# Router weights and routing masks with their low parts beside the high ones, in a macaron transformer layer

## What is computed

```
x = x + 0.5 * ffn(layernorm(x))
x = x + attention(layernorm(x))
x = x + 0.5 * ffn(layernorm(x))
```

```
gate_logits = einsum('bsd,ed->bse', x, gate_w)        # 8 logits a row
topw, sel = top_k(gate_logits, 2)
topw = softmax(topw, axis=1)                           # over the sequence axis
for e in range(8):
    c = sum(where(sel == e, topw, 0))
    h_e = silu(base_up + lo_up[e]) * (base_gate + lo_gate[e])
    mixed_h += c * h_e ;  lora_down += 2 * (c * h_e @ down_A[e].T @ down_B[e].T)
out = mixed_h @ w_down.T + lora_down
```

## Time and profile before

| | |
|---|---|
| median of 3 runs | 1437.02 us (1436.83 to 1437.51) |
| the profiled execution's own time | 1436.71 us |
| its span in the trace | 1434.9 us |
| PE busy | 1389.6 us (97%), 8164 matmuls |
| DVE, POOL, ACT busy | 1011.2 us (70%), 929.6 us (65%), 903.5 us (63%) |

### The profile page before, as it was taken

The page is one execution under the profiler, slowest core; times in us unless marked ns, Lnnn a source line. Parts: engine busy times, 40 slices in busy tenths (PEclk is TensorE's granted clock), DMA queues, the critical chain, the costliest instruction groups (busy, mean ns, idle before and its releaser), DMA issues.

```text
span 1434.9 us, 24075 instructions
## 1 busy us (share of the span) xinstructions
PE 1389.6 (97%) x8164; PEld 1214.6 (85%) x8164; DVE 1011.2 (70%) x2207; ACT 903.5 (63%) x1826; POOL 929.6 (65%) x818
## 2 busy tenths in 40 slices
PE   6999999889999999999999999999999988999998
PEld 4778888678999998998999899989999977878886
DVE  6877776867766766766766767766776788766665
ACT  4554443667777877777777767776776764544433
POOL 3665454477777877777777777777777744745543
PEclk9999999999999999999999999999999999999999
DMA  4000001000000000000000000000000030000000
GB/s 172 1 1 1 1 1 52 23 1 9 23 2 8 23 2 8 23 2 8 22 2 9 1 23 9 1 23 1 8 9 1 2 114 1 0 16 1 16 15 15
DMA packets 11415, 23.29 MB, mean 16 GB/s; under 512 B 928, under 2 KB 5024, under 8 KB 11168
## 3 DMA queue, kind: packets, MB, share of 16 engines
q1 hardware_dynamic: 11296, 21.78, 4.5%
HBM read 19.68 MB, written 2.10 MB: 15 GB/s over the span
## 4 chain that ended last, share of the span: by engine, by line
PE 85%; DVE 7%; POOL 4%; issue 2%; ACT 1%; DMA 0%; DVEq 0%; POOLq 0%; ACTq 0%
PE ps L1602 25%; PE ps L1604 25%; PE ps L1603 25%; PE ps L2011 8%; POOL um_l L356 1%; POOL hid_l L356 1%; DVE mixed L1218 1%; DVE hid L1208 1%; POOL w_l L356 0%; POOL mixed_l L356 0%; PE ps L1615 0%; DVE ps L1462 0%; DVE stats L1063 0%; DVE xn L1082 0%; DVE spread L1082 0%
## 5 line engine op out<-in xcount | busy, mean ns | idle before, releaser
L720 POOL TENSOR_SCALAR probs<-probs,inv_sum 128x128 f32<-128x128 f32 (+7 forms) x256 | 197.7, 776 | 210.6 <-DVE inv_sum L1447 210.6
L1462 DVE CUSTOM_DVE_ANT_0 ps<-ps,causal 128x128 f32<-128x128 f32 (+7 forms) x256 | 194.3, 759 | 125.1 <-PE ps L1604 124.7
L999 ACT ACTIVATE probs<-ps,neg_max 128x128 f32<-128x128 f32 (+7 forms) x256 | 189.4, 740 | 136.6 <-DVE neg_max L1462 136.3
L356 POOL TENSOR_TENSOR hid_l<-hid,hid_h 128x512 fp32r<-128x512 f32 x80 | 109.4, 1368 | 184.2 <-ACT hid_h L836 184.2
L2011 PE MATMUL ps<-ident,probs 128*128 128x128 f32 x1152 | 169.9, 274 | 7.6 <-DVE own_l L356 3.1
L704 POOL TENSOR_TENSOR rot_sin<-swapped,rope 128x512 f32<-128x512 f32 x128 | 165.5, 1293 | 17.8 <-ACT swapped L947 10.7
L710 POOL TENSOR_TENSOR rot<-rot,rot_sin 128x512 f32<-128x512 f32 x124 | 160.2, 1292 | 17.8
L2011 PEld LDWEIGHTS ps<-ident,probs 128*128 128x128 f32 x1152 | 133.1, 141 | 24.1 <-issue 3.8
L1602 PE MATMUL ps<-k_h,q_h 128*128 128x384 f32 (+5 forms) x384 | 151.0, 393 | 2.4 <-DVE q_l L356 2.4
L356 DVE TENSOR_TENSOR own_l<-ps,own_h 128x128 fp32r<-128x128 f32 (+3 forms) x256 | 124.0, 484 | 38.4 <-ACT own_h L970 38.4
L1604 PE MATMUL ps<-k_h,q_l 128*128 128x384 f32 (+5 forms) x384 | 131.3, 342 | 0.0
(11 more groups left out here) (202 smaller groups left out, 4396.1 us busy)
## 6 DMA issues: line engine op xcount, KB each, us to landing
w_raw<-attn_w SPq DMA_DIRECT2D x32, 256.0 KB, 2.9
w_in<-ffn_w SPq DMA_DIRECT2D x12, 576.0 KB, 9.2
x_sb<-x_in SPq DMA_DIRECT2D x4, 512.0 KB, 6.2
out<-x_sb SPq DMA_DIRECT2D x3, 512.0 KB, 3.1
rope<-rope_w SPq DMA_DIRECT2D x1, 1024.0 KB, 6.4
w_in<-ffn_w SPq DMA_DIRECT2D x2, 264.0 KB, 4.6
expand_raw<-expand_w SPq DMA_DIRECT2D x2, 256.0 KB, 5.8
out<-x_sb SPq DMA_DIRECT2D x2, 256.0 KB, 2.1
```

The lines of the kernel that those rows point to most:

```text
L356: return eng.tensor_tensor(dst, src, high.bitcast(F32), ALU.subtract)
L720: pool.tensor_scalar(probs[s % 4][:, 0:n], probs[s % 4][:, 0:n], inv_sum[:, s % 4:s % 4 + 1], 1.0, ALU.mult, ALU.mult).then_inc(probs_read ...
L999: act.activation(probs[t % 4][:, 0:a * n].rearrange("p (a n) -> p a n", a=a), view, ACT.Exp, bias=neg_max[:, t % 4:t % 4 + 1], scale=-1.0, ...
L1462: dve.tensor_tensor_reduce(out=view, in0=view, in1=causal[:, SEQ - a * n:].rearrange("p (a n) -> p a n", a=a), scale=-SCALE, scalar=HUGE, ...
```

## The change

The router's columns stand twice in block 0: 8 columns whose high part is kept, and the same 8 again, which POOL overwrites with the low part, for each half of the model dimension. A matmul then gives eight rows of high logits and eight of low logits at once, so that a chunk takes four matmuls instead of eight; `turn_logits` turns 16 rows, and a new DVE reduction adds the two halves into `cm` before the top eight are taken. The masks are put into `cm_pad` twice; the transpose gives 64 rows, of which the second 32 become the low part, in one tile `maskT`. C1 and C2 take one matmul each, with 64 rows of weights. M1 and D take one each as before, but with 32 rows of weights where there were 128.

```diff
-OFF_A = KT * EXPERTS
+OFF_A = KT * 2 * EXPERTS
...
         def w_route(w, kt):
-            at = OFF_ROUTE + kt * EXPERTS
+            at = OFF_ROUTE + kt * 2 * EXPERTS
             return w[:, at:at + P]
+        def route_parts(w):
+            return w[:, OFF_ROUTE:OFF_A].rearrange("p (a b e) -> p a b e", a=KT, b=2)[:, :, 1, :]
...
+                if n == 0:
+                    low(pool, route_parts(w_h), route_parts(w_in), route_parts(w_h))
+                    at = slice(OFF_A, BLOCK0)
                 low(pool, w_l[:, at], w_in[:, at], w_h[:, at]).then_inc(w_ready, 1)
...
                 dve.wait_ge(logits_ready, 2 * f + b + 1)
+                at = 2 * EXPERTS * SEQ_TILES * b
+                halves = ps[:, TURNED_BANKS[f][b], at:at + 2 * EXPERTS * SEQ_TILES]\
+                    .rearrange("p (t h e) -> p t h e", t=SEQ_TILES, h=2)
+                dve.tensor_reduce(cm[:, of_batch(b), 0:EXPERTS], halves.rearrange("p t h e -> p t e h"), AX.X, ALU.add)\
+                    .then_inc(logits_summed, 1)
+                dve.wait_ge(logits_summed, 2 * f + b + 1)
...
             def pad_mask(g, c):
                 need(dve, mask_turned, g)
-                dve.tensor_copy(cm_pad[:, :, 0:MASK_ROWS], cm[:, ds(CT * c, CT), :]).then_inc(cm_padded, 1)
+                twice = cm_pad[:, :, 0:2 * MASK_ROWS].rearrange("p t (k r) -> p t k r", k=2)
+                dve.tensor_copy(twice, cm[:, ds(CT * c, CT), None, :].to_broadcast([P, CT, 2, MASK_ROWS]))\
+                    .then_inc(cm_padded, 1)
             def mask_low_part(g, bank):
                 dve.wait_ge(mask_high, g + 1)
-                low(dve, maskT_l[:], ps[:, bank, :], maskT_h[:]).then_inc(mask_low, 1)
+                rest = maskT[MASK_ROWS:2 * MASK_ROWS]
+                low(dve, rest, ps[MASK_ROWS:2 * MASK_ROWS, bank, :], rest).then_inc(mask_low, 1)
...
                 for kt in range(KT):
-                    product(ps[:, bank, :], (w_route(w_h, kt), w_route(w_l, kt)), xnT(kt, chunk_cols(c)), kt == 0, False)
-                    ins = pe.matmul(ps[:, bank, :], w_route(w_l, kt), xnT_l[:, kt, chunk_cols(c)], start=False,
+                    pe.matmul(ps[:, bank, :], w_route(w_h, kt), xnT_h[:, kt, chunk_cols(c)], start=(kt == 0), stop=False)
+                    ins = pe.matmul(ps[:, bank, :], w_route(w_h, kt), xnT_l[:, kt, chunk_cols(c)], start=False,
                                     stop=(kt == KT - 1))
...
                 if e < EX_C1:
-                    pe.matmul(ps[:, banks[e], :], expand[:, e], maskT_h[:], start=True, stop=True).then_inc(spread_done, 1)
+                    pe.matmul(ps[:, banks[e], :], expand[0:MASK_ROWS, e], maskT[0:MASK_ROWS], start=True, stop=True)\
+                        .then_inc(spread_done, 1)
                 else:
                     pe.wait_ge(spread_kept, 4 * g + e - 1)
-                    pe.matmul(ps[:, banks[e], :], expand[:, e], maskT_h[:], start=True, stop=False)
-                    pe.matmul(ps[:, banks[e], :], expand[:, e], maskT_l[:], start=False, stop=True).then_inc(spread_done, 1)
+                    both = slice(0, 2 * MASK_ROWS)
+                    pe.matmul(ps[:, banks[e], :], expand[both, e], maskT[both], start=True, stop=True).then_inc(spread_done, 1)
```

More of the change, by code:

```diff
@@ L188, in build @@
             hid = sbuf(st, "hid", [P, 2, CHUNK])
-            sbuf(st, "before_values", [P, 48])
+            sbuf(st, "before_values", [P, 32])
             cm_pad = sbuf(st, "cm_pad", [P, CT, P])
@@ L199, in build @@
             spread = sbuf(st, "spread", [P, 2, 4, CHUNK])
-            maskT_h = sbuf(st, "maskT_h", [P, CHUNK], F32R)
-            maskT_l = sbuf(st, "maskT_l", [P, CHUNK], F32R)
+            maskT = sbuf(st, "maskT", [P, CHUNK], F32R)
+            sbuf(st, "mask_gap", [P, CHUNK])
             um_h = sbuf(st, "um_h", [P, 2, 4, CHUNK], F32R)
@@ L281, in build @@
         logits_ready = sem("logits_ready")
+        logits_summed = sem("logits_summed")
         route_chain = sem("route_chain")
@@ L358, in logitsT @@
         def logitsT(c):
-            return spread[0:EXPERTS, 1, c % 2, :]
+            return spread[0:2 * EXPERTS, 1, c % 2, :]
         def rope_low_part(eng, index, u, k):
@@ L772, in keep_logits @@
                 act.wait_ge(logitsT_done, 4 * f + c + 1)
-                act.activation(logitsT(c), ps[0:EXPERTS, LOGIT_BANKS[f][c], :], ACT.Copy).then_inc(logitsT_kept, 1)
+                act.activation(logitsT(c), ps[0:2 * EXPERTS, LOGIT_BANKS[f][c], :], ACT.Copy).then_inc(logitsT_kept, 1)
             def layer_norm_high(n, c, banks=(OUT0, OUT1), kts=range(KT)):
@@ L782, in mask_high_part @@
                 act.wait_ge(mask_turned, g + 1)
-                act.activation(maskT_h[:], ps[:, bank, :], ACT.Copy).then_inc(mask_high, 1)
+                act.activation(maskT[0:2 * MASK_ROWS], ps[0:2 * MASK_ROWS, bank, :], ACT.Copy).then_inc(mask_high, 1)
             def keep_spread(g, e, banks):
@@ L1106, in logits @@
                 def logits(tile):
-                    return ps[:, TURNED_BANKS[f][b], EXPERTS * tile:EXPERTS * tile + EXPERTS]
+                    return cm[:, tile, 0:EXPERTS]
                 dve.wait_ge(logits_ready, 2 * f + b + 1)
+                at = 2 * EXPERTS * SEQ_TILES * b
[4 more added lines that the diff above has]
+                dve.wait_ge(logits_summed, 2 * f + b + 1)
                 for tile in tiles:
@@ L1636, in turn_logits @@
                     for tt in range(CT):
-                        at = EXPERTS * (CT * c + tt)
-                        ins = pe.transpose(ps[:, TURNED_BANKS[f][b], at:at + EXPERTS], logitsT(c)[:, P * tt:P * tt + P],
-                                           ident[0:EXPERTS, 0:EXPERTS])
+                        at = 2 * EXPERTS * (CT * c + tt)
+                        ins = pe.transpose(ps[:, TURNED_BANKS[f][b], at:at + 2 * EXPERTS], logitsT(c)[:, P * tt:P * tt + P],
+                                           ident[0:2 * EXPERTS, 0:2 * EXPERTS])
                 ins.then_inc(logits_ready, 1)
@@ L1697, in turn_mask @@
                 for tt in range(CT):
-                    ins = pe.transpose(ps[:, bank, P * tt:P * tt + P], cm_pad[:, tt, :], ident[:])
+                    ins = pe.transpose(ps[0:2 * MASK_ROWS, bank, P * tt:P * tt + P], cm_pad[:, tt, 0:2 * MASK_ROWS], ident[:])
                 ins.then_inc(mask_turned, 1)
@@ L2141, in pack_ffn @@
     a = np.concatenate([up_A.reshape(ER, D).T, gate_A.reshape(ER, D).T], axis=1)
-    parts = [by_kt(gate_w.T), by_kt(a)]
+    parts = [by_kt(np.concatenate([gate_w.T, gate_w.T], axis=1)), by_kt(a)]
     for m in range(FULL):
@@ L2161, in expand_matrices @@
         m[EXPERTS + e, EX_D, ranks] = ALPHA
-        m[2 * EXPERTS + e, EX_C1, :] = 1.0
-        m[3 * EXPERTS + e, EX_C2, :] = 1.0
+        for part in (0, MASK_ROWS):
+            m[part + 2 * EXPERTS + e, EX_C1, :] = 1.0
+            m[part + 3 * EXPERTS + e, EX_C2, :] = 1.0
     return m.reshape(P, EX_COLS)
```

## The result

The changed kernel takes 1440.81 us (median of 10 runs, 1439.22 to 1441.21) beside 1436.76 us of the kernel before, measured with it (10 runs, 1435.96 to 1438.67). The ratio is 1.0026, 95% interval 1.0018 to 1.0034: slower by 4.05 us, clear of the noise, though the interval reaches down across the 0.2% that the prediction took as its line. The profiled execution took 1441.19 us, nearly the slowest of the ten, with a span of 1439.1, 4.2 more than the span of before.

What follows compares the result with a forecast made beforehand. PE was taken to bound the dense feed-forward stretches, with waits between engines at the two heads. The terms -2.23 - 1.86 + 4.41 + 0.14 made +0.46 us on 1437.02, so 1437.5 us, range 1430.0 to 1440.8.

Steps and rivals of the forecast that it cites:

- The likeliest case: Whole kernel: all terms as forecast, 1437.5 us, own range 1435.5 to 1439.0, chance 0.45; no change in all had 0.62.
- slower: Whole kernel above 1439.9 us, from dearer switches or the clock falling in both passes; chance 0.15.
- head of f = 0: First feed-forward pass's start: fewer router matmuls against a new reduction, copies and split subtraction; -2.23 us.
- head of f = 1: Second feed-forward pass's start: two groups of four router matmuls gain -0.93 us each, others vanish in waits; -1.86 us.
- spreads in six chunks: Inside six chunks: three excursions to fewer rows cost 1.20, two saved matmuls return 0.465; +0.735 each, +4.41 us.
- copy at chunk 1: Head of chunk 1, both passes: DVE's copy ahead of the second sequence's masks lies on the path; +0.14 us.
- The switches: PE in the chunks: changing between whole-array and fewer-row matmuls costs 0.20 us, there and back 0.40 us.
- free: Rival, spreads in the chunks: switches cost nothing, each chunk gains 0.465 us, total 1430.3 us; chance 0.14.
- half: Rival, spreads in the chunks: switches cost half, 18 x 0.20 us less, total 1433.9 us; chance 0.13.
- `router_logits(0, 3)` waits only 0.22 us and opens the dense stretch: Head of f = 0, last router product: four matmuls saved there count fully; -0.93 us.
- for the second sequence's reduction, DVE's own waits for PE in the dense stretches: Dense stretches: DVE's idle time hides the second reduction, cost 0; without this cover +0.27 us in each pass.
- The clock's rival: Both heads: longer PE waits drop the clock, slowing transposes and LoRA products; +1.2 to +3 us, 1438.7 to 1440.5, chance 0.20.

Runs made afterwards that it cites:

- run 3: The changed kernel with spreads inside the chunks over all 128 rows, zero-padded, still in one pass; 1433.82 us, ratio 0.9978 to the kernel before.
- run 8: The kernel before with M1 and D alone over 32 of 128 rows, no matmul removed; 1438.42 us, ratio 1.0008.
- run 12: The kernel before with both passes of C1 and C2 over 64 of 128 rows, no matmul removed; 1441.58 us, ratio 1.0033.
- Run 4: The changed kernel with PE waiting for the new reduction's end instead of the top-eight indices, in two places; 1437.79 us, ratio 1.0007 to the kernel before.
- run 11: The changed kernel plus 6 and 8 useless PE matmuls in waits at the two heads; 1438.76 us, ratio 1.0017 to the kernel before.
- run 5: The changed kernel with one-pass spreads over 128 rows and PE waiting for the reduction, not the indices; 1432.8 us, ratio 0.9971 to the kernel before.
- run 10: The kernel of run 5 plus 8 useless PE matmuls in the second head's wait alone; 1433.21 us, ratio 0.9969 to the kernel before.
- Run 6: The kernel before with eight more matmuls in a dense stretch (fourth chunk's M1 repeated), nothing else; 1438.65 us, ratio 1.0009.
- run 7: The kernel before with four more matmuls in the same dense stretch, nothing else; 1437.55 us, ratio 1.0003.
- both mends: The two edits of run 5 to the changed kernel: spreads over 128 rows, and PE waiting for the reduction; 1432.8 us.
- run 2: The kernel before with the changed masks and spreads alone, router as before; 1441.88 us, ratio 1.0035.
- run 1: The kernel before with the changed router alone, masks and spreads as before; 1434.56 us, ratio 0.9982.
- run 9: The kernel of run 5 plus 6 and 8 useless PE matmuls in waits at both heads; 1432.21 us, ratio 0.9967 to the kernel before.

## Why the prediction was right, and where it was not

The forecast of 1437.5 was 3.3 us low, and the time lies on the very edge of the range, which ended at 1440.8: that it falls inside is luck. The likeliest case said no change (0.62) and reached to 1439.0; what came was "slower", which had 0.15. The term that the prediction called decisive was right, the heads were not. By its own terms, against the two profiled executions:

| term | forecast | in the trace |
|---|---|---|
| head of f = 0 | -2.23 | -0.3 (0.53 at the landmark, less 0.735 for one chunk's spreads and 0.07 for the copy) |
| head of f = 1 | -1.86 | -1.7 (from 3.01 at 1177.74 to 2.14 at 1280.34, less 0.735 and 0.07) |
| spreads in six chunks | +4.41 | +4.49 (1.48 + 1.54 + 2 x 0.735) |
| copy at chunk 1 | +0.14 | taken as forecast |
| attention | 0 | +1.0 (from 2.01 at 218.64 to 3.01 at 1177.74) |
| end | 0 | +0.5 (3.68 at 1390.36 to 4.2) |
| sum | +0.46 | +4.2 |

**The switches: right, in mechanism and size.** "A switch takes some 0.09 us to let the array run empty and 0.11 us because the weights are loaded in the open", an excursion 0.40 us. Four ways of reading it agree: 1.10 us across C1 in after, 0.38 between run 3's landmarks, 0.375 from run 8's two chunks (0.75 / 2), and 1.32 us across C1 in run 12. It holds for 32 and 64 rows, though the price came from matmuls of 8 rows that are 8 columns long. That the price of such unlike matmuls would carry over this exactly was not known ahead (the bounds were 0 and 0.55); in part it is luck. The rivals "free" and "half" are excluded: run 12, which removes nothing and has 12 excursions, is 4.3 us slower, where half the price would make 2.4. The rule of the Trainium skill that the prediction named (TensorEngine Tiling (Array Packing), Key Properties), that a change of the tiling mode drains the engine, agrees with the traces at 32, 64 and 8 rows.

**The head of f = 0: the step that failed.** It is the term that priced eight matmuls at -1.86 and four at -0.93 "in the dense stretch" and let them count to the end. Up to `turn_mask` it held, though only against before's profiled execution (see the last section). Then it missed that the path leaves PE. First, "`router_logits(0, 3)` waits only 0.22 us and opens the dense stretch": what PE did earlier there, PE waited out at 53.32, since DVE's chain was released by products ahead of that router. Second, "for the second sequence's reduction, DVE's own waits for PE in the dense stretches" were named as its cover; there is none at this place, DVE works from 50.36 to 53.28 without a wait, and PE waits for the end. Run 4 takes the wait away and moves the landmark by 0.88 us. Third, the clock.

**The clock's rival (0.20): it came true in f = 0.** "The wait at 39.85 grows from 1.39", and the lower level behind it hits transposes and LoRA products: 1.25 us on DVE's path (run 11 against after), beside the 1.2 to 1.5 that the rival gave for one pass. The wait itself did not grow (1.39 us in both). In f = 1 it did not fall in after, but in run 3 it did. The traces of after and of runs 4 and 5 have this second low stretch, those of runs 3 and 10 don't, though they too have both parts of the change here; what decides it wasn't found. By the medians the router alone is 2.3 us faster and the spreads alone are 5.0 slower, which makes +2.6, and the whole change is +4.05. The other 1.4 us would fit this stretch and run 11 (-2.05), but they are not clear of the noise of three medians. In run 11's trace it is 1.25 us, and the rest of its lead over after comes from the start and from the attention.

**The head of f = 1: right** within 0.2 us. PE waited 1.87 us for DVE's rows (0.92 before), as said; it also waited 0.37 us for the second indices.

**What stays open.** In the profiled execution the attention and the last six matmuls (distance 0.21 instead of 0.12 us, granted clock 0.61) cost 1.5 us more. Runs 6 and 7 show that such a shift alone doesn't bring this cost in the median. What decides where the clock falls, at the first head as in the attention, wasn't settled. Nor was it tested what more than two matmuls of fewer rows in a row would cost.

## What to carry to other kernels

Fewer rows of weights are no saving for a lone matmul: padded with zeros to the shape of its neighbours, the same matmul is 0.4 us cheaper (512 columns, in a dense stretch). A saved matmul counts only if the engine that it is on sets the pace until the next place where all engines meet; ask of each head which engine releases the last wait, and which event that wait really needs (here the reduction, not the indices). And where a stretch with waits loses work, look at what the clock does behind it, in more than one execution: matmuls of no use in a wait were worth 1.25 us at one place of run 11's trace, and on the kernel with both mends nothing that the median could tell. Before you read the difference of two traces from their heads, compare each with other executions of the same code.

## What the runs showed of the hardware that I had not expected

**The level at the start differs between executions of the same code.** Run 6 has the instructions of the kernel before up to 166 us. Its first router products:

```profile
14.58 0.50 PE L1602 MATMUL ps<-xnT_h,w_h 128*128 128x512 f32 x1 [0.99 <-POOL w_l L356]
14.92 0.40 PE L1603 MATMUL ps<-xnT_l,w_h 128*128 128x512 f32 x1
15.15 0.39 PE L1604 MATMUL ps<-xnT_h,w_l 128*128 128x512 f32 x1
```

They stand 0.23 us apart (0.34 behind the first) where those of before's profiled execution had 0.43, so they ran at the higher level at once, and `turn_logits` at 20.11 instead of 21.79. Its landmark lies at 105.29 instead of 106.62. The column of the granted clock says 1.00 at 14 to 18 us in both, so only the distances show it. The Trainium skill, TensorE: Matmul & The Clock Gate, What's actually happening, says that the number of slow matmuls at a kernel's start varies from run to run: the traces agree.

Before and after both happened to start at the lower level, but for before that was the exception. Of the six profiled executions with the old router (before and runs 2, 6, 7, 8 and 12), five started at the higher level and had `turn_logits` at 20.04 to 20.13; only before's had it at 21.79. With the new router (after and runs 1, 3, 4, 5, 9, 10 and 11) it stands anywhere from 19.20 to 20.79, whichever level came first. Against those five executions after gains 0.4 us at this place, not 2.1, and the forecast's -1.86 there is not a typical gain: where the start is fast, PE waits for DVE's low parts instead (0.73 us in run 1), which the rows of before's slow start couldn't show. The landmark of before would then be near 105.3, and the failed step is larger than the table shows, by up to 1.3 us; how often before starts low among the runs behind its median, no trace tells.

**A shorter stretch of work can end later.** In run 1 the first two groups of router products had four matmuls less than in run 6 each, and both started at the higher level; yet `turn_logits` came at 20.63 against 20.11, because PE's wait at 15.9 to 16.6 was followed by the lower level.
